# An index sort given to the list scheduler, and the destination rows' norm ranked above the dense blocks, in a four-layer graph network kernel

## The reference, cut to what matters

```python
x = _layernorm(x + _L0_gnn_ref(x, ...))     # attention: softmax of edge scores per destination
x = _layernorm(x + _L1_gnn_ref(x, ...))     # attention, gelu, norm, MLP 64 -> 128 -> 64, norm
x = _layernorm(x + _L2_gnn_ref(x, ...))     # segment_sum over src of x[dst], weights from degrees
x = _layernorm(x + _L3_gnn_ref(x, ...))     # segment_sum over dst of weight * x[src]

# layer 0 and 1, the scores: a part of the source row plus a part of the destination row
logits = e @ attn                                        # e from x[src], edge_attr and x[dst]
att_scores = x_src @ att_w[:D] + x[dst] @ att_w[D:]
e = jnp.exp(att_scores - seg_max[dst]); att = e / segment_sum(e, dst)[dst]
```

## Time and profile before

| | us |
|---|---|
| median of three runs | 2754.26 |
| the profiled execution | 2762.78 |
| its span, first to last instruction | 2760.7 |
| around the span | 2.1 |
| PE, DVE, ACT, POOL busy | 1812.3, 1724.6, 1489.0, 1673.6 |
| share of the span | 66%, 62%, 54%, 61% |
| mean granted TensorE clock | 0.825 |

### The profile page before, as it was taken

One profiled execution on the slowest core, in us unless ns is written; L12 is line 12 of the kernel. 1 busy time (PEld: TensorE's weight loads), 2 busy tenths in 40 slices (PEclk: granted clock), 3 DMA queues, 4 the chain that ended last, 5 costly groups with the idle time before them and its releaser, 6 DMA issues. The chain is left out here.

```text
span 2760.7 us, 24755 instructions
## 1 busy us (share of the span) xinstructions
PE 1812.3 (66%) x7450; PEld 857.1 (31%) x7450; DVE 1724.6 (62%) x3288; ACT 1489.0 (54%) x2240; POOL 1673.6 (61%) x1610
## 2 busy tenths in 40 slices
PE   5998788679988989888999877568773253000000
PEld 3444334223643343333444323443221142000000
DVE  4886699998988888785555449997663285000002
ACT  3777567557678877877877756348773021000000
POOL 6777777700047772001777757776777788777774
PEclk9999999889999989999999979659996555555555
DMA  3223222203632221122444483432210133000002
GB/s 67 67 68 82 49 64 64 51 31 95 206 108 60 70 63 41 48 61 71 131 138 138 119 214 113 124 97 72 58 55 25 49 110 108 15 17 21 22 21 97
DMA packets 236807, 214.81 MB, mean 78 GB/s; under 512 B 157821, under 2 KB 170964, under 8 KB 236676
## 3 DMA queue, kind: packets, MB, share of 16 engines
q1 hardware_dynamic: 182228, 166.60, 21.3%
q0 software_dynamic: 51200, 46.31, 6.9%
q10 hardware_dynamic: 3248, 0.34, 0.1%
HBM read 140.36 MB, written 86.31 MB: 82 GB/s over the span
## 5 line engine op out<-in xcount | busy, mean ns | idle before, releaser
L2385 POOL DMA_INDIRECT stab<-wk,rank_i x200 | 212.0, 1060 | 320.6 <-DVE wk L595 263.9
L552 ACT ACTIVATE b_s<-ps,vec 128x512 f32<-128x512 f32 (+1 forms) x356 | 241.6, 683 | 137.4 <-PE ps L546 58.0
L2382 POOL DMA_INDIRECT e_bc<-x0tab,dpos_i x136 | 136.6, 1005 | 282.9 <-DVEq L2183 241.8
L2382 POOL DMA_INDIRECT u<-x2tab,dpos_i x200 | 224.4, 1122 | 87.4 <-issue 83.7
L783 DVE TENSOR_SCALAR b_x<-b_s 128x8 f32<-128x8 f32 x2 | 0.3, 168 | 416.9 <-DMA b_gl<-out_dram 416.9
L2382 POOL DMA_INDIRECT u<-x3tab,src_i x200 | 203.0, 1015 | 76.0 <-issue 58.2
L2382 POOL DMA_INDIRECT u<-in_x_dram,src_i x200 | 201.0, 1005 | 76.8 <-issue 58.5
L2382 POOL DMA_INDIRECT u<-in_x_dram,dst_i x200 | 204.2, 1021 | 65.1 <-issue 60.8
L2385 POOL DMA_INDIRECT out_dram<-u,sfin_i x200 | 197.0, 985 | 66.3 <-issue 66.3
L2385 POOL DMA_INDIRECT out_dram<-u,dst_i x176 | 201.7, 1146 | 56.3 <-issue 56.3
L535 PE MATMUL ps<-b_h,wt 64*128 64x512 f32 (+1 forms) x296 | 178.5, 688 | 38.3 <-DVE b_x L694 33.7
(11 more groups left out here) (424 smaller groups left out, 4742.1 us busy)
## 6 DMA issues: line engine op xcount, KB each, us to landing
b_gl<-in_x_dram SPq DMA_DIRECT2D x98, 256.0 KB, 2.8
wk<-dlist SPq DMA_DIRECT2D x50, 500.0 KB
wk<-slist SPq DMA_DIRECT2D x50, 500.0 KB
out_dram<-b_gl SPq DMA_DIRECT2D x93, 256.0 KB
u<-stab SPq DMA_DIRECT2D x25, 510.0 KB
x2none<-b_gl SPq DMA_DIRECT2D x25, 250.0 KB
x0tab<-e_bc SPq DMA_DIRECT2D x25, 240.0 KB
wk<-x2none SPq DMA_DIRECT2D x25, 240.0 KB
```

The source lines that it names most:

```text
L552: return nc.scalar.activation(b_s[l][:, 0:w], pB[l][:, 0:w], ACT.Abs_reciprocal_sqrt, bias=col(EPSV))
L2382: pool.indirect_dma_start(out=o, out_offset=None, in_=tab, in_offset=at_ix(ix), **kw).then_inc(s, 16)
L2385: pool.indirect_dma_start(out=tab, out_offset=at_ix(ix), in_=a, in_offset=None, bounds_check=last, oob_is_err=False).then_inc(s, 16)
```

## The change

The table `IX`, `BUSY`, `slow`, `reserve` and `held` are gone. The index sort becomes a unit `ix` of rank 1: 422 DVE steps `s0` to `s421` with assumed durations, each dependent on the one before, and the PE steps `h1` to `h4`, `cb_a` to `eb_b` with their turns on bank `e1`. `index_dve`, `index_pe` and `index_sp` take their times from the plan. `packed` and `ordered` depend on steps of `ix`, and so does `u2` of group 17. The unit `xd1` gets rank 1 instead of 2. No operation is added or taken away. What changes is the order in each engine's list, and for some dense blocks which of ACT and DVE moves a bank out (steps `u` and `out`, which the scheduler gives to either): DVE has 17 more of these.

```diff
-        IX = dict(sort1=62, join=232, h1=239, h2=254, keys=269, cb=281, la=293, fb=305, nb=317, eb=329, derive=341, undo=368,
-                  h3=384, h4=402, out=410, pack=416, sort2=424, end=602)
...
-        unit(("packed", 0), 0, f"t sp {IX['sort2'] + 8}")
-        unit(("ordered", 0), 0, f"t sp {IX['end'] - IX['sort2']}", [(("packed", 0), "t", 0)])
+        index_us, index_text = [], []
+
+        def on_dve(*us, marks=""):
+            for k, t_us in enumerate(us):
+                index_text.append(f"s{len(index_us)} dve {t_us}" + (marks if k == 0 else ""))
+                index_us.append(t_us)
+
+        def on_pe(name, us, marks=" +e1"):
+            index_text.append(f"{name} pe {us}{marks}")
+
+        def sort_us(ts_us, stage_us, copy_us, stt_us, turn_us):
+            out = [ts_us] + [stage_us] * 36
+            for m in range(7):
+                out.append(ts_us)
+                for bit in range(m, 4, -1):
+                    out += [copy_us * (64 >> bit), stt_us, ts_us]
+                out += [turn_us] + [stage_us] * (min(m, 4) + 1) + [turn_us] + [stage_us] * 8
+            return out
+
+        on_dve(1.7, .8, 1.1, *sort_us(.4, .6, .5, .55, .5), .8, .8, .8, .9, .9, .6)
+        index_at = dict(join=len(index_us))
+        landed = {f"s{len(index_us)}": 7.0}
+        on_dve(.9, 1.2, 1.2)
+        for h in ("h1", "h2"):
+            on_pe(h, .7)
+            on_dve(.8, *[1.2] * 7, marks=" -e1")
+        index_at["keys"] = len(index_us)
+        on_dve(.1)
+        landed[f"s{len(index_us)}"] = 0.0
+        for name, us in (("cb", 3.5), ("la", 3.1), ("fb", 4.0), ("nb", 3.1), ("eb", 4.6)):
+            if name == "fb":
+                landed[f"s{len(index_us)}"] = 1.0
+            on_dve(us, .3)
+            on_pe(name + "_a", .9)
+            on_dve(1.4, marks=" -e1")
+            on_pe(name + "_b", .6)
+            on_dve(.8, marks=" -e1")
+        on_dve(1.5, 1.5, 1.3, 1.5, 1.5, 1.4, 1.5, 1.1, 1.2, 1.2, 1.4, .8, 1.4, 1.2, 1.4)
+        on_dve(*[.55, .55, .9] * 7)
+        on_pe("h3", .7)
+        on_dve(.8, *[.55, .55, .9] * 7, marks=" -e1")
+        on_pe("h4", .7)
+        on_dve(.8, *[.55, .55, .9] * 2, marks=" -e1")
+        index_at["freed"] = len(index_us) - 1
+        on_dve(1.2, 1.3, .4, 1.0, .8, 1.1, 1.1, 1.2, 1.3, .9)
+        index_at["packed"] = len(index_us) - 1
+        on_dve(*sort_us(.6, .82, .9, .85, .8), 1.1, .1)
+        index_at["end"] = len(index_us) - 1
+        unit(("ix", 0), 1, ";".join(index_text), **{k: [(("ix", 0), f"s{int(k[1:]) - 1}", us)] for k, us in landed.items()})
+        unit(("packed", 0), 0, "t sp .1", [(("ix", 0), f"s{index_at['packed']}", 3.0)])
+        unit(("ordered", 0), 0, "t sp .1", [(("ix", 0), f"s{len(index_us) - 1}", 4.0)])
...
-            unit(("u2", g), 0, "t pool 10.7", [(("u2", g - 1) if g else ("u1", NG - 1), "t", 0)])
+            unit(("u2", g), 0, "t pool 10.7", [(("u2", g - 1) if g else ("u1", NG - 1), "t", 0)] +
+                 ([(("ix", 0), f"s{index_at['freed']}", 0)] if g == FIRST_MASKED else []))
...
-            unit(("xd1", g), 2, "a dve 1.4;sq act .65;var dve .7;rs act .3;mul dve .7;dot dve 1.45",
+            unit(("xd1", g), 1, "a dve 1.4;sq act .65;var dve .7;rs act .3;mul dve .7;dot dve 1.45",
...
-        BUSY = ((IX["sort1"], IX["join"], 2.4), (IX["join"], IX["sort2"], 1.8), (IX["sort2"], IX["end"], 2.2))
...
-                        if r == "e1":
-                            for a, z in held:
-                                if a - 4.5 < t < z:
...
-                    us = us * slow(eng, t) + switch(eng, name)
+                    us = us + switch(eng, name)
...
-            clk, step = [IX["sort1"]], [0]
-
-            def tick(dt):
-                clk[0] += dt
-                return clk[0]
-
-            def until(name):
-                assert clk[0] <= IX[name], (name, clk[0])
-                clk[0] = IX[name]
-                return clk[0]
+            planned, taken, step = at["ix", 0], [-1], [0]
+
+            def tick(dt=None):
+                taken[0] += 1
+                return planned[f"s{taken[0]}"]
```

More of the change, by code:

```diff
@@ L345, in gnn_resnorm_kernel @@
         uses = {"e0": [], "e1": []}
-        held = []
         on = {}
@@ L1707, in index_sp @@
         def index_sp(sp):
+            t_ix = at["ix", 0]
+            t_join, t_keys, t_packed, t_end = (t_ix[f"s{index_at[k]}"] for k in ("join", "keys", "packed", "end"))
             yield 1
@@ L1746, in index_sp @@
             sp.dma_start(f3(ix_tile["kn"]), flat4(klist, 2)).then_inc(S("keys_in"), 16)
-            yield IX["out"] + 5
+            yield t_packed - 3
             sp.wait_ge(S("index_made"), 2)
@@ L1756, in index_sp @@
             sp.sem_inc(S("index_out"), 1)
-            yield IX["end"] + 1
+            yield t_end + .5
             sp.wait_ge(S("index_made"), 4)
@@ L1936, in index_dve @@
             a, b = JOIN
-            yield until("join")
+            yield tick()
             dve.wait_ge(S("ix_b"), 32)
@@ L1945, in index_dve @@
             for hop, h in ((0, "h1"), (1, "h2")):
-                yield until(h)
                 for j in (64, 32, 16, 8, 4, 2, 1):
@@ L1956, in index_dve @@
                     a, b, level = b, a, level + 1
-            yield until("keys")
+            yield tick()
             X = ix_tile
@@ L1993, in whole @@
                 nc.vector.nop().then_inc(S("e1_free"), 1)
-            yield until("cb")
+            yield tick()
             k_i = X["t"].bitcast(i32)
@@ L2001, in index_dve @@
             yield from whole(0, X["cb"], False, ALU.add)
-            yield until("la")
+            yield tick()
             ts(X["t"], X["isb"], -1.0, 1.0, ALU.mult, ALU.add)
@@ L2006, in index_dve @@
             yield from whole(1, X["la"], False, ALU.max)
-            yield until("fb")
+            yield tick()
             dve.wait_ge(S("keys_in"), 32)
@@ L2013, in index_dve @@
             yield from whole(2, X["fb"], False, ALU.max)
-            yield until("nb")
+            yield tick()
             ts(X["t"], X["ka"], -1.0, BIGK, ALU.mult, ALU.add)
@@ L2018, in index_dve @@
             yield from whole(3, X["nb"], True, ALU.max)
-            yield until("eb")
+            yield tick()
             tt(X["t"], X["ka"], X["kn"], ALU.not_equal)
@@ L2025, in index_dve @@
             yield from whole(4, X["eb"], True, ALU.max)
-            yield until("derive")
+            yield tick()
             t, t2, valid, q, deg = X["t"], X["kp"], X["kn"], X["nb"], X["eb"]
@@ L2064, in index_dve @@
             ts(a.bitcast(i32), wi, 1 << 30, None, ALU.bitwise_or)
-            yield until("undo")
             level = MASKS - 1
@@ L2071, in index_dve @@
                     if first:
-                        yield until("h3")
                         yield tick(1.5)
@@ L2079, in index_dve @@
                     a, b, level = b, a, level - 1
-            yield until("h4")
             yield tick(1.5)
@@ L2091, in index_dve @@
             W = b.bitcast(i32)
-            yield until("out")
+            yield tick()
             wi = w_[6].bitcast(i32)
@@ L2100, in index_dve @@
             nc.vector.nop().then_inc(S("index_made"), 1)
-            yield until("pack")
+            yield tick()
             ei = w_[8][:, 0:256].bitcast(i32)
@@ L2121, in index_dve @@
             ready()
-            yield until("end")
+            yield tick()
             nc.vector.nop().then_inc(S("index_made"), 1)
+            assert taken[0] == len(index_us) - 1, (taken[0], len(index_us))
         def prep2_sp(sp, t, k):
```

48 lines of the change are left out of this document (17 added, 31 removed).

## The result

| | before | after |
|---|---|---|
| median, four runs each | 2753.11 | 2679.17 |
| lowest to highest | 2746.59 to 2765.38 | 2675.15 to 2680.65 |
| profiled execution | 2762.78 | 2680.65 |
| its span | 2760.7 | 2678.8 |
| mean granted TensorE clock | 0.825 | 0.829 |

The ratio of the runs is 0.9724 (95% interval 0.9694 to 0.9754): faster by 74 us in medians, 82 us in the profiled executions (before's profiled one lay 9.7 us above its median, after's 1.5). Forecast were 94 us in the sum and 2662; it is 17 us slower than that and inside the range.

What follows compares the result with a forecast made beforehand. POOL's two long waits, before the `x0tab` gathers and the record scatters, were taken to set the end. Terms -40 + 5 - 55 - 3 - 1 = -94 us gave 2660 on the median, stated as 2662, range 2625 to 2708.

Steps and rivals of the forecast that it cites:

- the two gaps of POOL: POOL's waits of 241.8 us before the first `x0tab` gather and 241.0 before the first record scatter; shortening them advances the end.
- Part 1: Up to softmax 0: the sort in the scheduler fills idle DVE time; addition at 565, 40 us gained (12 to 50).
- over 90%: Sign that the forecast is right: DVE busy for more than this share from 100 us on.
- Rival (a): Early stretch gives nothing, as sort steps hold up `l0` and `l0d`; softmax 0 near 593, total 2702; chance 0.12.
- The rule against it: Fuller DVE slows POOL's gathers: some 6 us later by the trace, some 10 by the skill's shared-port rule.
- Part 2: Softmax 0 to `u3`: 70 more sort instructions on DVE, 25 fewer of dense blocks; +5 us (0 to 11).
- PE sets the pace there: Softmax 0 to `u3`: PE busy 173.6 of 187 us, so DVE's extra 11 us lie mostly beside it.
- Part 3: First `u3` gather to softmax 1: `xd1` sums ahead of dense blocks; 318 us, a gain of 55 (33 to 90).
- Part 4: Softmax 1 to the end: -3 us to the first record, -1 for records, postponed dense blocks cost nothing.
- Rival (c): Slower: postponed blocks crowd PE from `u5` to the scatters; all gain lost below clock 0.55, 2827 at 0.5; chance 0.04.
- Rival (d): PE or DVE lags in layer 2 and returns 60 to 70 us; 2727 and up; chance 0.05.
- Rival (b): Larger gain, some 120 us: softmax 0 at 556, last score close behind its last gather; 2634; chance 0.11.

Runs made afterwards that it cites:

- sort_only: The changed kernel with `xd1` back at rank 2, so only the sort's move into the scheduler is left; 2725.64 us, ratio 0.9894 to the kernel before.
- xd1_only: The kernel before with `xd1` at rank 1 instead of 2, the sort's fixed times kept; 2698.86 us, ratio 0.982 to the kernel before.
- held_rank1: The changed kernel, `xd1` at rank 1, with no dense block allowed to begin between the end of `prep2` and the last source-group score; 2629.64 us, ratio 0.9555.
- dense_held: The changed kernel with `xd1` back at rank 2 and no dense block beginning between the end of `prep2` and the last source-group score; 2621.62 us, ratio 0.9511.
- fill1: The changed kernel with one more 128x500 matmul, its result unused, in each of the 25 source groups; 2686.5 us, ratio 0.9768 to the kernel before.
- held_m2: `dense_held` with dense blocks also kept out during the sums of layer 2, up to its last `main` group; 2613.33 us, ratio 0.9486 to the kernel before.

## Why the prediction was right, and where it was off

**What bounds the kernel.** Right. The gain lies in the two gaps of POOL, and the end followed: the final scatters began at 2097.70 (about 2083 was named), without long waits before or within them. That the total of -82 lies so near to -94 is in part luck: the parts missed by 16, 4.6 and 4.5 us one way and by 7.6 and 6.3 the other.

**Part 1** forecast 565 (555 to 593); it came at 557.87. The floor, the last gather and what `l0d` takes behind it, was worked out right and was reached; that gather started 3.2 us later than before (551.81 against 548.64). I had kept 10 us for a DVE that would still be late. DVE was 265.9 + 183.4 = 449 us busy ahead of the addition, of 461 forecast, and in the second window only 88%, not the "over 90%" that I named. Rival (a), a softmax 0 near 593, did not come true, here or in `sort_only` (560.76).

**The rule against it.** With 41 us more of DVE work in 44 to 350 (the prediction had 31, without a working), POOL issued 230 transfers in this window, and 231 before; one `u2` gather took 1.038 us on average instead of 1.021, and the last started 3.2 us later. One pair of traces is too little here, though: over the twelve runs with the sort in the scheduler the last `u2` gather starts between 550.4 and 559.1, and in before and `xd1_only`, which have the same order up to softmax 0, at 548.6 and 544.3. The means differ by 7 us, which lies between the 6 us worked out from the rows and the 10 us worked out from the rule of the Trainium skill ("SBUF — State Buffer", "Who interferes with whom"), and decides for neither. Nor is it shown that DVE is the cause: the `u1` gathers, beside which DVE was busy 216.0 instead of 187.1 us, took 262.8 us from first to last after and 262.6 before; the `u2` gathers, 270.7 and 268.1. The gathers' durations after:

```profile
L2402 POOL DMA_INDIRECT u<-in_x_dram,dst_i x200 | 207.7, 1038 | 64.3 <-issue 60.9 <-DMA u<-in_x_dram,dst_i 3.0 <-DMA u<-in_x_dram,src_i 0.3
```

**Part 2** forecast +5 (0 to 11); it was +9.6, inside the bounds, but "PE sets the pace there" failed for the first half. Between 616 and 658 PE was 29.5 of 42 us busy at a clock of 0.67; before, in the like window of 33 us (666 to 699), 30.4 at 1.00. The last cast of the second sort came at 649.94, 92 us behind the addition, instead of 8. `xd1_only`, where the sort stands as before, kept 185.9 us: so the 9.6 us come with the sort's move. Whether by its DVE instructions or by the clock is open; with the sort at rank 0 both were a bit better and there was no gain.

The window of after between:

```profile
616.00:658.00 42.00, 29.50 (x167) 18.87 (x167) 36.59 (x70) 13.54 (x19) 0.00 (x0) 0.67 0.45 135
```

**Part 3** forecast -55 (33 to 90); it was -39.0. The mechanism was right: all `xd1` sums stand ahead of the last score, and the rank alone gives 45 us in `xd1_only` and 51 between `sort_only` and after (384.6 to 333.8). The term that was mis-sized is the last score, put at about 317 us behind the first gather, from the count of DVE instructions, since "DVE has room". It came at 332.5: 6 us because the gathers took 268.8 instead of 262.6, the other 10 because it lagged behind the last gather by 65.2 us from start to start instead of some 55. The 6 us are four pauses of POOL of 1.8 to 2.0 us each, between 899 and 991, where before the gaps stay under 0.6; three of them end 0.8 us behind an addition of `x1s` (line 1200) that reads a tile the gathers write, so the lag seems to have held up the gathers too, though the profile names no releaser. DVE did have room, 66 us of it; what the source groups lacked at the start was a lane. The count of 20 fewer dense instructions looked like a relief, and was read without asking how long each block left in the stretch would keep what it holds. `held_rank1` shows the price: 50 us.

**Part 4** forecast -3, -1 and 0 for the backlog. The backlog is there: from the last record to the final scatters DVE was busy 431.1 us instead of 389.4, 42 more, of 46 forecast, and PE 438.8 instead of 377.3, 62 more, of 79. In the last window it was 179.6 instead of 132.7 and 220.1 instead of 155.5. The stage from `u6` to the scatters grew by 3 us. `u6` was held up by 15.2 instead of 12.3 us. The records gained 7.3 instead of 1: a wait of 9.8 us before the second group's records is gone, and from the last record to `u5` it takes 19.0 instead of 23.4 us; against these stand slower issues. Rival (c) would have needed a clock below 0.55 there; it was 0.98 where the backlog ran. Rival (d) asked for 60 to 70 us lost in layer 2; `u5` to `u6` lost 3.5.

**Rival (b)**, 2634 with the score close behind its gather, did not come true in the change but is what `dense_held` made: lag 20.1 us, 2621.62. I had given it 0.11 with the lag of before against it; the lag of before was not that of the chain alone, but also of the blocks that shared its lanes.

## What to carry to other kernels

When a list scheduler gets a new rank order, ask not only how much low-rank work stands in a stretch but what each begun piece of it holds (here a lane of PSUM) and how long it keeps it when everything else outranks it: raising `xd1` gained 45 us and at the same time made two blocks hold their lanes for 81 and 65 us, where `sort_only` took 45 and 39. Filler is best kept from starting in a stretch whose latency counts, and done beside a queue that sets the time by itself: 65 us more of PE's work beside the last gathers cost 3 us here. A stage's engine shares (80% here) do not show this; the lag from a group's last gather to its result does, and so does the time from a group's being ready to its head.

## What was not expected of the hardware

The granted clock, a mean over two levels (1.2 and 2.4 GHz, 0.5 and 1.0 here), could not be read off PE's busy share. In the stretch it was 0.84 after with PE 79% busy (263.65 of 334), 0.96 in `dense_held` with PE 80% (222.75 of 278) and 0.86 in `fill1` with 82%. Nor did a lower clock mean a longer stage: 0.65 in `held_m2` went with a stage that was 10 us shorter than in `dense_held` at 0.77, PE being busy 160 of 295 us instead of 202 of 304. What the clock took from the stretch after, where it was 0.84, no run shows.
